# Identity products on TensorE where its steps wait for operands, in a four-layer attention and expert kernel

## The reference

```python
x = x + _L0_xattn_ref(_layernorm(x), ctx, ctx, ...)      # 16 heads of 8
x = x + _L0_ffn_ref(_layernorm(x), ...)                  # self attention, 8 heads of 64, experts for v and o
x = x + _L1_xattn_ref(_layernorm(x), ctx, 32, ...)       # one head, the 32 best scores of 77
x = x + _L1_ffn_ref(_layernorm(x), ...)                  # causal grouped attention, then 8 experts, the best 2
x = x + _L2_xattn_ref(_layernorm(x), ctx)                # one head
x = x + _L2_ffn_ref(_layernorm(x), ...)                  # fake-quantized gate, up and down products
x = x + _L3_xattn_ref(_layernorm(x), ctx, ...)           # 16 heads of 8, masked
x = x + _L3_ffn_ref(_layernorm(x), ...)                  # relu, width 512
```

## Time and profile before

| | us |
|---|---|
| median of 3 runs | 1599.28 |
| the runs | 1594.57 to 1600.89 |
| the profiled execution | 1593.11 |
| its span (first to last instruction) | 1591.4 |
| mean granted clock of TensorE in the span | 0.835 |

### The profile page before, as it was taken

The page is one execution under the profiler, slowest core; times in us unless marked ns, Lnnn a source line. Parts: engine busy times, 40 slices in busy tenths (PEclk is TensorE's granted clock), DMA queues, the critical chain, the costliest instruction groups (busy, mean ns, idle before and its releaser), DMA issues. The chain is left out here.

```text
span 1591.4 us, 35682 instructions
## 1 busy us (share of the span) xinstructions
PE 1223.7 (77%) x13690; PEld 910.2 (57%) x13691; DVE 1075.5 (68%) x2504; ACT 849.7 (53%) x2714; POOL 808.7 (51%) x825
## 2 busy tenths in 40 slices
PE   2788978869777887987887787887534388988986
PEld 1566766655655675765666565564420166766664
DVE  2456786887887777886687888775534786544542
ACT  1787765545558477469376465545233323454442
POOL 2138586696576459437738747642204322433432
PEclk9576877978989998889887889799865576998998
DMA  5000000000000000000000000010002000000000
GB/s 153 5 2 1 1 1 1 2 1 1 20 1 9 12 2 1 20 2 1 20 2 1 1 1 16 9 44 1 8 22 55 1 1 2 9 9 15 9 8 15
DMA packets 26977, 19.48 MB, mean 12 GB/s; under 512 B 6552, under 2 KB 24248, under 8 KB 26680
## 3 DMA queue, kind: packets, MB, share of 16 engines
q1 hardware_dynamic: 26808, 17.20, 3.8%
HBM read 13.00 MB, written 4.19 MB: 11 GB/s over the span
## 5 line engine op out<-in xcount | busy, mean ns | idle before, releaser
L1047 ACT ACTIVATE arena<-bank 128x512 f32<-128x512 f32 (+5 forms) x361 | 186.2, 546 | 266.0 <-PE bank L431 76.4
L1446 DVE TENSOR_REDUCE arena<-pair 128x8 f32<-128x1024 f32 (+2 forms) x224 | 241.2, 1095 | 118.5 <-PE pair L476 46.7
L2059 POOL TENSOR_SCALAR_AFFINE_SELECT arena<-arena 128x1024 f32<-128x1024 f32 (+1 forms) x128 | 146.7, 1160 | 304.1 <-ACT arena L1415 176.3
L2114 POOL TENSOR_TENSOR arena<-arena 128x512 f32<-128x512 f32 x160 | 185.4, 1159 | 45.1 <-DVE arena L1563 38.0
L1094 ACT ACTIVATE arena<-pair,arena 77x128 f32<-77x128 f32 x512 | 178.4, 372 | 33.6 <-DVE arena L1446 28.9
L2119 POOL TENSOR_TENSOR arena<-arena 128x512 f32<-128x512 f32 x128 | 180.9, 1413 | 10.0
L431 PE MATMUL bank<-ident,arena 128*128 128x128 f32 (+1 forms) x352 | 68.0, 326 | 82.9 <-ACT arena L1055 21.8
L2135 POOL TENSOR_TENSOR arena<-arena 128x512 f32<-128x512 f32 x64 | 67.0, 1065 | 116.0 <-ACT arena L1047 69.8
L1415 ACT ACTIVATE arena<-pair 77x1024 f32<-77x1024 f32 x64 | 62.6, 1014 | 112.6 <-PE pair L977 109.6
L1094 ACT ACTIVATION_READ_ACCUMULATOR arena<-pair,arena 77x1 f32 x512 | 109.6, 214 | 0.0
L1047 ACT ACTIVATE arena<-bank,arena 128x128 f32<-128x128 f32 x256 | 77.5, 496 | 52.4 <-PE bank L800 34.8
(11 more groups left out here) (289 smaller groups left out, 3017.1 us busy)
## 6 DMA issues: line engine op xcount, KB each, us to landing
arena<-in_ctx_turned SPq DMA_DIRECT2D x16, 154.0 KB, 2.5
arena<-in_x SPq DMA_DIRECT2D x8, 256.0 KB, 5.4
spill<-arena SPq DMA_DIRECT2D x8, 256.0 KB, 2.0
arena<-spill SPq DMA_DIRECT2D x8, 256.0 KB, 2.6
out<-arena SPq DMA_DIRECT2D x8, 256.0 KB, 2.4
arena<-in_ctx SPq DMA_DIRECT2D x8, 154.0 KB
arena<-in_ctx_turned SPq DMA_DIRECT2D x1, 1232.0 KB, 6.1
wexp<-in_L_ffn_expert_w SPq DMA_DIRECT2D x1, 512.0 KB, 4.5
```

The source lines that it names most:

```text
L1047: return act.activation(dst, src, func, bias=bias, scale=scale)
L1446: return dve.tensor_reduce(dst, src, X, op, **kw)
L2059: return pool.affine_select(out=e, in_=e, compare_op=ALU.is_ge, fill=0.0, base=0, pattern=[[0, 8], [1, 128]], channel_multiplier=-1)
L2114: pool.tensor_tensor(into, xvs[:, b, ex * SHD:(ex + 1) * SHD].unsqueeze(1).broadcast_to([128, SH, SHD]), gates[g % 2][:, b, 0:SH, ex].unsq ...
```

## The change

Each step of TensorE in stages A and C now takes its place in the ring and waits for the bank first. Then it calls a new function `keep`, which puts into that bank as many products of the 128x128 fp32 identity with itself as a new table `FILL` says for this use of this step: a digit, 0 to 9, one for each use over the 8 groups. Then it waits for the operands and runs its own products, which start their accumulation anew, so that nothing of the identity products is left. In `f0t` the wait for the probabilities moves in the same way into the loop over the two halves. The digits sum to 409, in 140 of the 1052 steps. `ORDER` is unchanged, stage B is unchanged, and so are the programs of all other engines: the lists of instructions of DVE (1588 rows), ACT (670), POOL (693) and SP (85) are as long as before.

```diff
+FILL = {
+    "weights0": "70000000",
...
+    "f0t0": "1000005000100000401010300010404000000000200010000040000000102020",
+    "f0v0": "20010400500000002001000000000622",
...
+    "m10": "54203029",
+    "m11": "30010002",
+    "m12": "00000000",
+    "m13": "0000000030000000000000000000000000000000000000000000000090000000",
+    "m14": "00400039",
...
+    "x3s0": "30000000000000000000100000000000",
...
+    "f30": "21373129",
+    "f31": "00001000000000000000000010002000",
+    "f32": "00000002",
+}
...
+            uses = {}
+
+            def keep(o, step):
+
+                k = uses[step] = uses.get(step, -1) + 1
+                for _ in range(int(FILL[step][k])):
+                    mm(o.bank[:, 0:128], ident[:], ident[:], start=True, stop=True)
...
                 yield
+                o = E.take("x0", g, "n")
+                pe.wait_ge(o.drained, o.n)
+                keep(o, "x0p1")
                 pe.wait_ge(ln0.n, C.next(ln0.n))
-                o = E.take("x0", g, "n")
-                pe.wait_ge(o.drained, o.n)
                 transpose4(o, n0).then_inc(o.full, 1)
...
                     for pairs_of in units("x0"):
                         yield
+                        o = take_pairs("x0", g, pairs_of, lambda p: (2 * b + p,))
+                        keep(o[pairs_of[0]], "x0s0")
                         if b == 0 and 0 in pairs_of:
...
-                        o = take_pairs("x0", g, pairs_of, lambda p: (2 * b + p,))
...
             def f0t(g):
                 for b in range(SEQS):
-                    yield
-                    p = S["f0", g, "s", b]
-                    pe.wait_ge(p.drained, p.n + 1)
                     for p in range(2):
-                        if p:
-                            yield
+                        yield
                         o = E.take("f0", g, "pT", b, p)
                         pe.wait_ge(o.drained, o.n)
+                        keep(o, "f0t0")
+                        e = S["f0", g, "s", b]
+                        pe.wait_ge(e.drained, e.n + 1)
```

More of the change, by code:

```diff
@@ L435, in x0p @@
                 yield
+                o = E.take("x0", g, "k")
+                pe.wait_ge(o.drained, o.n)
+                keep(o, "x0p0")
                 pe.wait_ge(ctx0_in[g % 2], 16 * (g // 2 + 1))
@@ L453, in x0p @@
                 yield
+                o = E.take("x0", g, "q")
+                pe.wait_ge(o.drained, o.n)
+                keep(o, "x0p3")
                 n = E["x0", g, "n"]
@@ L483, in x0v @@
                     yield
+                    o = E.take("x0", g, "av", b)
+                    pe.wait_ge(o.drained, o.n)
+                    keep(o, "x0v0")
                     pe.wait_ge(x0_v, C.next(x0_v))
@@ L496, in x0v @@
                 yield
+                o = E.take("x0", g, "o")
+                pe.wait_ge(o.drained, o.n)
+                keep(o, "x0v1")
                 for b in range(SEQS):
@@ L513, in f0p @@
                     yield
+                    o = E.take("f0", g, "xv", b)
+                    pe.wait_ge(o.drained, o.n)
+                    keep(o, "f0p1")
                     if b == 0:
@@ L539, in f0s @@
                     yield
+                    o = S.take("f0", g, "s", b)
+                    pe.wait_ge(o.drained, o.n)
+                    keep(o, "f0s1")
                     for name in "qk":
@@ L602, in x1 @@
                 yield
+                o = E.take("x1", g, "k")
+                pe.wait_ge(o.drained, o.n)
+                keep(o, "x10")
                 pe.wait_ge(ctx_in[g % NCTX], 32 * (g // NCTX + 1))
@@ L668, in f1p @@
                     yield
+                    o = E.take("f1", g, name)
+                    pe.wait_ge(o.drained, o.n)
+                    keep(o, "f1p1")
                     n = E["f1", g, "n"]
@@ L712, in f1t @@
                     yield
+                    o = E.take("f1", g, "nm", b)
+                    pe.wait_ge(o.drained, o.n)
+                    keep(o, "f1t0")
                     for p in range(2):
@@ L743, in f1v @@
                     yield
+                    o = E.take("f1", g, "av", b)
+                    pe.wait_ge(o.drained, o.n)
+                    keep(o, "f1v0")
                     if b == 0:
@@ L765, in f1v @@
                 yield
+                o = E.take("f1", g, "o")
+                pe.wait_ge(o.drained, o.n)
+                keep(o, "f1v1")
                 for b in range(SEQS):
@@ L840, in kv3 @@
                 yield
+                o = E.take("kv", g, "k")
+                pe.wait_ge(o.drained, o.n)
+                keep(o, "kv30")
                 if g == 0:
@@ L858, in weights @@
                     yield
+                    o = E.take("centred", i)
+                    pe.wait_ge(o.drained, o.n)
+                    keep(o, "weights0")
                     if name == "f1":
@@ L914, in x3p @@
                 yield
+                o = E.take("x3", g, "n")
+                pe.wait_ge(o.drained, o.n)
+                keep(o, "x3p0")
                 if g == 0:
@@ L952, in x3t @@
                     yield
+                    o = E.take("x3", g, "nm", b)
+                    pe.wait_ge(o.drained, o.n)
+                    keep(o, "x3t0")
                     for p in range(2):
@@ L984, in x3v @@
                     yield
+                    o = E.take("x3", g, "av", b)
+                    pe.wait_ge(o.drained, o.n)
+                    keep(o, "x3v0")
                     if b == 0:
@@ L1006, in x3v @@
                 yield
+                o = E.take("x3", g, "o")
+                pe.wait_ge(o.drained, o.n)
+                keep(o, "x3v1")
                 for b in range(SEQS):
@@ L1023, in f3 @@
                     yield
+                    o = E.take("f3", g, "h", t)
+                    pe.wait_ge(o.drained, o.n)
+                    keep(o, "f31")
                     if t == 0:
```

210 lines of the change are left out of this document (128 added, 82 removed).

## The result

The changed kernel takes 1576.35 us (median of 4 runs, 1574.04 to 1579.88) and the kernel before 1597.38 us (4 runs, 1594.57 to 1600.89): a ratio of 0.9853, 95% interval 0.9816 to 0.9891. The profiled execution has a span of 1575.9 us at a mean granted clock of 0.881 (before 0.835), so PE ran at 1.2 GHz (slow time, from here on) for (1 - 0.881) x 2 x 1575.9 = 375 us, 150 us less than the 525 us before.

A forecast was written before the change was run, and what follows sets the result against it. No engine was full; TensorE was busiest at 77%, idle 367.7 us in waits, with 525 us at half clock. Product cost +3, stage A -7 and stage C -9 gave -13 from 1599.3: 1586 us, range 1558 to 1606.

The forecast's parts named there:

- Cost of the products: At the filled steps of stages A and C: products exceeding their waits delay steps, +3 us, bounds 0 and +22.
- Slow time: Over the whole span: TensorE's time at 1.2 GHz falls by 100 of 525 us, mean clock about 0.867.
- the end of stage A: Last chain of stage A: products too few to bring the clock back, 0 taken, bound -10 us.
- What stage A gives: Stage A: 66 us less time at half clock, at 0.1 for each, gives -7 us.
- The price of 0.1 for a slow microsecond: Stage A: each microsecond at half clock loses 0.09 by DVE's busy shares, 0.115 by ACT's, nothing by POOL's.
- What stage C gives: Stage C: 23 x 0.32 + 13 x 0.1 for less time at half clock, -9 us.
- The term for the order of the waits: At the changed steps: waits that change places cost nothing, since both already came before the first product.
- The penalty in the Trainium skill: Whole kernel: throttled time costs half at this level, so 100 us less would give -50 us, about 1552.
- The rival in which the clock feeds itself: Outside the end of A and stage B: fewer falls shorten slow spells, -40 us, 1562 us; chance 0.15.
- The rival in which delays win: Stage A's `f0t`, `f0o`, `f0v` steps: products delay them, making the kernel slower, 1605 to 1613 us; chance 0.15.
- the stretch behind 319 us: Stage A, first fall examined: the stretch from 315 to 319 us would no longer be followed by clock 0.50.
- The third rival's sign: Stage A: clock 0.86, `f0t`, `f0o`, `f0v` steps starting right behind their products, ACT's waits for TensorE longer; chance 0.15.

The follow-up runs named there:

- the second set: Runs of stage C's products alone, the changed kernel with and without 96 products, and the tuned table, against the kernel before rerun; changed kernel: ratio 0.9805.
- the tuned table: Changed kernel with 1139 identity transposes at 106 steps, sized to about 80% of each step's wait, instead of 409 products; ratio 0.9748 to the kernel before, 1563.1 us.

## Why the prediction was right, and where its terms were off

The sign and the mechanism held. Without products there is no gain. With products that take PE as long but do little for the clock there is a loss. With full products or transposes, the time falls roughly as the clock rises. The forecast was 13 us below the 1599.3 us of before, and 21 were measured (31 in the second set). The measured 1576.35 us lies inside the whole range, but just below the 1577 to 1595 that the forecast had for itself. That it came so near is in part luck: the gain of stage A and the cost of the products were both put too low, and the two errors work against each other.

- **Cost of the products: +3 us forecast; more was paid, but how much depends on the price of the clock.** The step "eight products of 128x128 take 1.06 us" failed: x8 in the earlier trace rows are four products of two records. One product costs (1.06 - 0.60) / 2 = 0.23 us at full clock, so all 409 are about 94 us and not 47, and 49 steps instead of 26 start right behind theirs. PE's busy time rose by 65 us where the prediction had it "nearly unchanged". The run with 32-row products lost 9.5 us outright, 20 with its clock counted at 0.25. The changed kernel itself gives 174 x 0.25 - 31 = 12 us in the second set, but nothing at the 0.17 of the tuned table.
- **Slow time: 100 us less forecast, 150 in the trace, 174 in the medians over the runs of the second set.** In stage A 66 us were forecast and 95 measured up to 1135 us, from 6 stretches fewer and shorter ones. Of the 36 us that were forecast for stage C, most came (about 35 by the two-digit clocks of stages B and C). The rest is the end of stage A, where 0 was taken: there the clock comes back in the long waits, and 3 us are gained. That each product was twice as long as thought helped here: half the amount gave half the gain in clock.
- **What stage A gives: -7 us forecast, -4 with the cost; -11 to -24 net measured.** That is the whole gain of 21 or 31 us without stage C's 7 to 10, and it takes in the 3 us of the stage's end. The price of 0.1 for a slow microsecond was the term that failed. Comparing DVE's busy share in slow and fast stretches compares different work: it cannot tell how late the same work would be. Executions of one program with different clocks come nearer to that, and one pair gives about 0.4 for stage A.
- **What stage C gives: -9 us forecast, 7 to 10 in the traces.** Here periods of the same work had been compared, and the term was right.

The term for the order of the waits (nothing) was right. The penalty in the Trainium skill that the prediction weighed (TensorE: Matmul & The Clock Gate, Terms), half of the throttled time, is not borne out for the time of this kernel: 0.20 to 0.39 us here by the slopes, 0.17 by the tuned table. The rival in which the clock feeds itself is not told from the forecast's own mechanism by any run; a time near its 1562 us was reached, but with a clock of 0.90 and a larger table, not through the present digits. The rival in which delays win is what the run with 32 rows shows, at 1.0059: its mechanism is real, its place was right in part, and it lost because the delays came with more clock than they cost. In that rival's working half of 47 us is 23.5 and not 22, which moves its 1613 by 2 us and changes nothing.

Of the signs that the prediction named, the clock (0.881), the stretch behind 319 us and four of the five periods of stage C (one takes 35.9 us) came close. The trace has 43 slow stretches, where 36 to 42 were forecast. PE's busy time and the end of stage A did not come as forecast. The third rival's sign, steps that start right behind their products, came as well.

## What to carry to other kernels

Where TensorE waits for operands in a fixed order of steps, and the clock falls after such waits, take the output bank first and fill the wait with full-array products or transposes, sized from the wait and less than it: in one set the first table gave 2.0% (1.5% in its first comparison), and one made from the waits of the filled kernel 2.5%. Price the clock by several executions of the same program, not by busy shares within one, and do not expect the price to hold when much of the slow time is gone. Where whole runs scatter by 1%, compare a part of the program that repeats better from trace to trace (here stages B and C, within 0.6 us in two traces). Count records against the program's own number of products before multiplying a duration.

## What the runs showed of the hardware

- In this kernel's traces an fp32 product of 128 columns is two records and 0.23 us at full clock, a transpose one record and 0.115 us.
- Products over 32 rows take as long as over 128 (mean 328 and 312 ns per record), but the clock was 0.840 with them (0.827 without any) and 0.881 with full ones.
- Two fp32 transposes of the identity kept the clock as well as one product (0.880 and 0.881).
- The same kernel varied between 1589.9 and 1611.0 us in one set, with its clock between 0.815 and 0.838. The slower runs mostly had the lower clock; which of the two drives the other is not shown.
